# Audio tower on one core: patches embedded without their norm, which a rank-two term adds behind the product

## The reference

```python
x = layer_norm(x, g1, b1, 1e-6)              # 448 rows x 1024
x = einsum('bpd,dh->bph', x, W) + b          # W: 1024 x 512
h = layer_norm(x, g2, b2, 1e-6)
h = h + attention(_layernorm(h))             # 16 heads of 128, causal
h = h + ffn(_layernorm(h))                   # rows rounded to fp8, 512 x 512
```

## Time and profile before

| | |
|---|---|
| median of 3 runs | 266.8 us (266.61 to 266.83) |
| profiled execution, its own time | 268.16 us |
| its span, first to last instruction | 266.4 us |
| PE busy | 256.4 us (96%) |
| DVE busy | 159.5 us (60%) |
| ACT busy | 124.8 us (47%) |
| mean granted TensorE clock | 0.991 |

### The profile page before, as it was taken

One profiled execution on the slowest core, in us unless ns is written; L12 is line 12 of the kernel. 1 busy time (PEld: TensorE's weight loads), 2 busy tenths in 40 slices (PEclk: granted clock), 3 DMA queues, 4 the chain that ended last, 5 costly groups with the idle time before them and its releaser, 6 DMA issues.

```text
span 266.4 us, 3864 instructions
## 1 busy us (share of the span) xinstructions
PE 256.4 (96%) x1434; PEld 219.8 (83%) x1434; DVE 159.5 (60%) x325; ACT 124.8 (47%) x215; POOL 0.2 (0%) x4
## 2 busy tenths in 40 slices
PE   7799999899899999999999999999999999999994
PEld 6344446898799999999999999999999999998672
DVE  5268996833926903872394269138722967934884
ACT  2666964354534542534362435325443642546680
POOL 0000000000000000000000000000000000000000
PEclk9999999999999999999999999999999999999888
DMA  6999030033071053023305210530240020000004
GB/s 180 332 277 387 11 119 0 2 123 113 0 253 65 2 197 118 1 60 137 118 0 171 64 80 0 197 118 0 43 153 0 2 79 0 2 0 0 0 4 138
DMA packets 7627, 23.63 MB, mean 89 GB/s; under 512 B 1261, under 2 KB 1725, under 8 KB 7488
## 3 DMA queue, kind: packets, MB, share of 16 engines
q1 hardware_dynamic: 7616, 23.48, 26.9%
HBM read 22.56 MB, written 0.92 MB: 88 GB/s over the span
## 4 chain that ended last, share of the span: by engine, by line
PE 88%; DMA 4%; DVE 3%; SPq 2%; issue 1%; ACT 1%; DVEq 0%; ACTq 0%
PE bank L315 14%; PE bank L317 14%; PE bank L316 14%; PE acc L459 9%; PE acc L350 9%; PE bank L434 5%; PE bank L443 5%; PE acc L463 4%; DMA tokw_raw<-tok_w 4%; PE acc L653 3%; PE bank L449 3%; PE bank L426 2%; SPq L248 2%; PE bank L523 2%; PE bank L639 1%; PE bank L339 1%
## 5 line engine op out<-in xcount | busy, mean ns | idle before, releaser
L315 PE MATMUL bank<-ht_hi,qkvw_hi 128*128 128x448 f32 (+1 forms) x192 | 69.4, 362 | 0.9 <-issue 0.9
L317 PE MATMUL bank<-ht_hi,qkvw_lo 128*128 128x448 f32 (+1 forms) x192 | 69.1, 360 | 0.0
L316 PE MATMUL bank<-ht_lo,qkvw_hi 128*128 128x448 f32 (+1 forms) x192 | 69.0, 359 | 0.0
L948 DVE TENSOR_TENSOR qkvw_lo<-raw_qkv,qkvw_hi 128x1536 fp32r<-128x1536 f32 x16 | 28.1, 1754 | 35.6 <-ACT qkvw_hi L685 35.6
L315 PEld LDWEIGHTS bank<-ht_hi,qkvw_hi 128*128 128x128 f32 x192 | 36.1, 188 | 3.9 <-issue 1.3
L317 PEld LDWEIGHTS bank<-ht_hi,qkvw_lo 128*128 128x128 f32 x192 | 36.1, 188 | 2.7
L316 PEld LDWEIGHTS bank<-ht_lo,qkvw_hi 128*128 128x128 f32 x192 | 36.1, 188 | 2.6
L350 PE MATMUL acc<-tokw_raw,xt 128*112 128x512 f32 x64 | 29.7, 600 | 1.7 <-DMA tokw_raw<-tok_w 1.3
L685 ACT CAST qkvw_hi<-raw_qkv 128x1536 fp32r<-128x1536 f32 x16 | 23.5, 1477 | 0.0
L350 PEld LDWEIGHTS acc<-tokw_raw,xt 128*112 128x112 f32 x64 | 10.4, 176 | 15.4 <-issue 9.6
L1154 DVE COPY prob_t<-bank 112x448 f32<-112x448 f32 x8 | 5.0, 625 | 29.0 <-PE bank L426 29.0
(11 more groups left out here) (148 smaller groups left out, 396.5 us busy)
## 6 DMA issues: line engine op xcount, KB each, us to landing
raw_qkv<-heads_w SPq DMA_DIRECT2D x16, 768.0 KB, 4.3
raw_out<-heads_w SPq DMA_DIRECT2D x16, 256.0 KB, 4.5
tokw_raw<-tok_w SPq DMA_DIRECT2D x4, 512.0 KB, 7.4
x_in<-patches SPq DMA_DIRECT2D x3, 448.0 KB, 11.2
ffnw_raw<-ffn_w SPq DMA_DIRECT2D x1, 1024.0 KB, 16.4
out<-h_sb SPq DMA_DIRECT2D x3, 224.0 KB, 2.6
x_in<-patches SPq DMA_DIRECT2D x2, 224.0 KB, 3.0
g_row<-tok_g SPq DMA_DIRECT2D x1, 224.0 KB, 10.7
```

What stands on the lines that cost most here:

```text
L315: nc.tensor.matmul(ps, hi, whi, start=first, stop=False, skip_group_check=True)
L316: nc.tensor.matmul(ps, hi, wlo, start=False, stop=False, skip_group_check=True)
L317: return nc.tensor.matmul(ps, lo, whi, start=False, stop=last, skip_group_check=True)
L948: return nc.vector.tensor_tensor(dst, src, hi.bitcast(F32), ALU.subtract)
```

## The change

The patches are no longer normalised before the product. With m and s the mean and the deviation of a row, the embedding times s is

    (x g1) W  -  m (g1 W)  +  s (b1 W + b)

so PE turns the raw patches, ACT lays only g1 on, and the two last terms are added by one more product, of a column of row statistics with two rows of gains (`recentre`). What stands in `acc[t]` is the embedding times s; the next norm takes that factor out again, its epsilon being scaled by s squared (`x_eps_4`).

- **Gains.** Two spare columns of `xt` hold g1 and b1 for tile 0 (`SPARE` = 114 rows in the product), so that rows 112 and 113 of `acc[0]` become g1 W and b1 W; `gains_done` adds b to the latter. They are kept in high and low parts (`gains_hi` on ACT, `gains_lo` on VectorE).
- **Statistics.** -m (ACT) and s (VectorE) of two tiles at a time are laid into `stat_cols`, turned by PE (`stat_transposes`) and split as well (`stat_hi`, `stat_lo`). The roots of the patches' variances are taken for two tiles at a time (`patch_roots`), and `patch_sigmas` on VectorE waits for them.
- **Order.** The loads, and the work of the front on all engines, stand in another order. Every rsqrt now starts from a root of ACT, and each tile's second and third norm are made in one go (`stream_norms(t)`). The warm-up products at the start are 6 and 2 rather than 14.

```diff
-WARM_START, WARM_STATS, WARM_RSTD, WARM_SCALE = 14, 2, 3, 3
+WARM_START, WARM_STATS, WARM_RSTD, WARM_SCALE = 6, 2, 3, 3
...
+SPARE = TR + 2
+G_ROW, G_AGAIN, G_LO = 96, 64, 32
+STAT_COLS = slice(G_LO + TR - 96, 128, 32)
+SIGMA_COLS = slice(G_LO + TR - 96 + 1, 128, 32)
...
-            for c, landed in ((slice(0, 512), x_landed[0]), (slice(512, IN_DIM), x0_rest_landed)):
-                load(x_in[:, 0, c], patches[0][:, c], landed)
+            load(x_in[:, 0, 0:512], patches[0][:, 0:512], x_landed[0])
             load(ident_sb[:], ident, ident_landed)
             load(g1_col[:], tok_g1, cols_landed)
+            load(x_in[:, 0, 512:IN_DIM], patches[0][:, 512:IN_DIM], x0_rest_landed)
+            load_tokw(0)
             load(b1_col[:], tok_b1, cols_landed)
-            load_tokw(0)
+            load_tokw(1)
+            load_tokw(2)
             load(tok_b_raw[:], tok_b, tok_b_landed)
-            load_tokw(1)
+            load_tokw(3)
             load(x_in[:, 1, :], patches[1], x_landed[1])
-            load_tokw(2)
-            load_tokw(3)
             load(x_in[:, 2, :], patches[2], x_landed[2])
             load(x_in[:, 3, :], patches[3], x_landed[3])
...
-                    pe.wait_ge(x0_half_normed, 1)
-                else:
-                    pe.wait_ge(x_normed, t + 1)
+                pe.wait_ge(x_landed[t], 16)
...
-            def embed(t, half, within=None):
-                for k in range(half * KIN // 2, (half + 1) * KIN // 2):
+            def embed(t, ahead_of):
+                m = SPARE if t == 0 else TR
+                if t == 0:
+                    pe.wait_ge(spare_ok, 2)
+                if t == TILES - 1:
+                    pe.wait_ge(stat_lo_ok, 2)
+                for k in range(KIN):
+                    if k in ahead_of:
+                        ahead_of[k]()
                     for i, (first_chunk, _) in enumerate(TOKW_PIECES):
                         if t == 0 and k == first_chunk:
                             pe.wait_ge(tokw_landed[i], 16)
                     pe.wait_ge(xt_ok, KIN * t + k + 1)
-                    nc.tensor.matmul(acc[t][0:TR, :], xt[:, t % 2, k * TR:(k + 1) * TR], tokw_raw[:, k, :],
+                    nc.tensor.matmul(acc[t][0:m, :], xt[:, t % 2, k * SPARE:k * SPARE + m], tokw_raw[:, k, :],
                                      start=(k == 0), stop=False, skip_group_check=True)
...
+            def gains_done():
+                pe.wait_ge(tok_b_lo_ok, 1)
+                pe.wait_ge(ones_ok, 3)
+                nc.tensor.matmul(acc[0][0:SPARE, :], bias_row[:], tok_b_split[:], start=False, stop=False,
+                                 skip_group_check=True).then_inc(gain_ps, 1)
+            def stat_transposes(pair):
+                pe.wait_ge(sigma_ok, pair + 1)
+                pe.wait_ge(negmean_ok, pair + 1)
+                if pair == 1:
+                    pe.wait_ge(stat_lo_ok, 1)
+                for t in range(2 * pair, 2 * pair + 2):
+                    last = nc.tensor.transpose(acc[TILES - 1][:, t * TR:(t + 1) * TR], stat_cols[:, t, :],
+                                               ident_sb[0:TR, 0:TR])
+                last.then_inc(stat_ps, 1)
+            def recentre(t):
+                pe.wait_ge(gain_lo_ok, 1)
+                pe.wait_ge(stat_lo_ok, t // 2 + 1)
+                nc.tensor.matmul(acc[t][0:TR, :], stat_t[:, t, :], gain_rows[:], start=False, stop=True,
+                                 skip_group_check=True).then_inc(tok_ps, 1)
...
-            pe.wait_ge(ones_ok, 2)
+            pe.wait_ge(ones_ok, 1)
             keep_warm(WARM_START, acc[TILES - 1])
             patch_transposes(0)
-            for t in range(TILES):
-                embed(t, 0)
-                if t == 0:
-                    embed(t, 1, within=lambda: patch_transposes(1))
-                    continue
-                if t + 1 < TILES:
-                    patch_transposes(t + 1)
-                else:
-                    stream_transposes(1)
-                embed(t, 1)
-                if t == TILES - 2:
-                    stream_transposes(0)
+            keep_warm(2, acc[TILES - 1])
+            embed(0, {KIN - 2: lambda: patch_transposes(1)})
+            gains_done()
+            embed(1, {2: lambda: stat_transposes(0), 4: lambda: patch_transposes(2), 6: lambda: recentre(0)})
+            recentre(1)
+            embed(2, {2: lambda: stat_transposes(1), 4: lambda: patch_transposes(3)})
+            recentre(2)
+            stream_transposes(0)
+            embed(3, {4: lambda: stream_transposes(1)})
+            recentre(3)
             stream_transposes(2)
...
+            def patch_evacuate(t, half):
+                act.wait_ge(xt_ps, 2 * t + half + 1)
+                if t == 2 and half == 0:
+                    act.wait_ge(gain_ps, 1)
+                if t == 3 and half == 0:
+                    act.wait_ge(tok_ps, 2)
+                for k in range(half * KIN // 2, (half + 1) * KIN // 2):
+                    nc.scalar.mul(xt[:, t % 2, k * SPARE:k * SPARE + TR],
+                                  bank[2 * (t % 2) + half][:, k % 4 * TR:(k % 4 + 1) * TR],
+                                  g1_col[:, k:k + 1]).then_inc(xt_ok, 1)
+            def patch_roots(pair):
...
+                nc.scalar.activation(root[:, t], moments[:, t, 1], ACT.Sqrt, bias=eps_4[:, 0:1],
+                                     scale=0.25).then_inc(x_root_ok, 1)
+                act.wait_ge(cleared, 3)
+                nc.scalar.mul(stat_cols[:, t, STAT_COLS], moments[:, t, 0:1].to_broadcast([TR, 2, 3]),
+                              -1.0).then_inc(negmean_ok, 1)
...
-            take_root(0)
-            normalise(0, slice(IN_DIM // 2, IN_DIM))
+            act.wait_ge(eps_ok, 2)
+            nc.scalar.activation(last_root[:, 0:1], eps_4[:, 0:1], ACT.Sqrt)
             act.wait_ge(cols_landed, 32)
-            patch_evacuate(0)
+            patch_evacuate(0, 0)
+            patch_evacuate(0, 1)
             act.wait_ge(tok_b_landed, 16)
             hi_part(tok_b_split[:], tok_b_raw[:]).then_inc(tok_b_hi_ok, 1)
-            take_root(1)
-            normalise(1)
-            patch_evacuate(1, between=lambda: take_root(2))
-            normalise(2)
-            take_root(3)
-            take_root(TILES)
-            normalise(3)
-            patch_evacuate(2)
+            patch_evacuate(1, 0)
+            patch_roots(0)
+            patch_evacuate(1, 1)
+            gains_hi()
+            stat_hi(0)
+            patch_evacuate(2, 0)
+            patch_evacuate(2, 1)
+            patch_roots(1)
+            token_root(0)
+            stat_hi(1)
             split_qkv(0, 0)
+            stream_root(0)
+            normalise_stream(0)
+            token_root(1)
+            patch_evacuate(3, 0)
+            patch_evacuate(3, 1)
+            stream_root(1)
+            stream_evacuate(0)
+            normalise_stream(1)
             split_qkv(0, 1)
+            token_root(2)
+            stream_evacuate(1)
+            stream_root(2)
+            normalise_stream(2)
             split_out(0, 0)
-            normalise_stream(0)
-            take_root(2 * TILES + 1)
-            patch_evacuate(3)
-            stream_evacuate(0)
-            take_root(TILES + 2)
-            normalise_stream(1)
-            stream_evacuate(1)
-            take_root(2 * TILES + 2)
-            normalise_stream(2)
+            token_root(3)
             stream_evacuate(2)
-            take_root(TILES + 3)
             keep_stream(2)
             act.wait_ge(late_landed, 64)
             hi_part(ffn_b_split[:], ffn_b_raw[:]).then_inc(ffn_b_hi_ok, 1)
-            take_root(2 * TILES + 3)
+            stream_root(3)
             stream_evacuate(3)
...
+            def rsqrt_from_root(c, minus_v4):
+                v, y, n = vscaled[:, c:c + 1], rstd[:, c:c + 1], newton[:, c:c + 1]
+                link(nc.vector.reciprocal(y, root[:, c:c + 1]))
+                need(minus_v4)
+                link(nc.vector.scalar_tensor_tensor(out=n, in0=y, scalar=v, in1=y, op0=ALU.mult, op1=ALU.mult))
+                link(nc.vector.scalar_tensor_tensor(out=y, in0=n, scalar=3.0, in1=y, op0=ALU.add, op1=ALU.mult))
...
+            def patch_sigmas(pair):
+                t = slice(2 * pair, 2 * pair + 2)
+                dve.wait_ge(x_var_ok, 2 * pair + 2)
+                nc.vector.tensor_scalar(x_eps_4[:, t], moments[:, t, 1], LN_EPS, 4.0 * LN_EPS,
+                                        ALU.add, ALU.mult).then_inc(x_eps_ok, 1)
+                dve.wait_ge(x_root_ok, pair + 1)
+                link(nc.vector.reciprocal(sigma_rec[:, t], root[:, t]))
...
+            def stream_norms(t, between=None):
+                c, p = TILES + t, 2 * TILES + t
+                dve.wait_ge(tok_ps, t + 1)
+                moments_of(c, [acc[t][0:TR, :]], tok_var_ok)
+                dve.wait_ge(tok_var_ok, t + 1)
+                centred_step = mark(nc.vector.scalar_tensor_tensor(
```

(44 more changed lines are left out.)

235 lines of the change are left out of this document (83 added, 152 removed).

## The result

The changed kernel takes 272.6 us (median of 4 runs, 270.68 to 274.64) against 266.81 of before; ratio 1.0187, interval 1.0138 to 1.0236. It is slower, as forecast, and by 5.8 us where 2.0 were forecast. The four executions lie in two pairs, 270.68 and 271.11 at a mean granted clock of 0.998 and 0.999, and 274.09 and 274.64 at 0.987. The profiled one is of the first pair: 271.11 us, span 269.2.

A forecast was written before the change was run, and what follows sets the result against it. PE, busy 256.4 of 266.4 us, was taken as the bound, with only the front changing. PE's and the norms' paths met at 51.1 against 49.18: +2.0 on the 266.8 median gave 268.8 us, range 267.4 to 270.6.

The forecast's parts named there:

- The train of norms: VectorE's norms of tiles 0 to 3 in the front: start at 26.6 us instead of 21.90, 4.7 later.
- Lengths: VectorE's time in the norms of tiles 0, 1 and 2: 6.1, 6.3 and 6.6 us.
- PE's wait behind `recentre(3)`: PE stands idle 1.5 us before turning tile 2 of the stream, at 45.9 to 46.0 instead of 43.38.
- From landing to the end of the front: PE's and the norms' paths meet at 51.1 against 49.18: +1.9 to +2.0 us up to line 523.
- PE's added work: One more `recentre` product (0.59) and statistics transposes (0.4) in the front: PE alone +0.9 us.
- Rival 1: Only PE's added work in the front shows: +0.9, 267.7 us; chance 0.08.
- The landing of tile 1: Tile 1's patches, loaded behind all of W, land at 15.64, where W's fourth piece did; the rearrangement gains 0.1 us.
- Taking 1.4 us off both sides: Whole-kernel time: the profiled execution lay 1.4 above the median, so 270.2 became a median of 268.8 us.
- PE ready for tile 1 by then: Front: first product by about 8.5, tile 0 with over 2 us to spare before tile 1 lands.
- b1's column, put at nothing: Front loads: landing behind W's first piece, it holds back the first copies, yet the first product starts by about 8.5.
- Rival 3: PE runs tile 0's products at 1.2 GHz after the shorter warm-up: +3.1 on top, 271.9 us; chance 0.09.
- The loop: The loop over heads behind the front keeps its order, so the front's gain or loss is the whole change.

The follow-up runs named there:

- b_again1: Kernel before the change, run again unchanged for a profile: 267.22 us.
- e4: Changed kernel with the norms brought forward: PE finishes accumulator 0 before turning tile 2, VectorE norms tile 0 before later patch statistics; 269.39 us, ratio 1.0052.
- e8: Changed kernel with only the VectorE and ScalarE half of e4's reordering, PE's order kept: 271.54 us, ratio 1.0125.
- e3: Changed kernel with b1's column loaded ahead of W's first piece: 271.7 us, ratio 1.0168.
- e6: Changed kernel with the edits of e3 and e4 together: 270.0 us, ratio 1.0065.
- e10: e6 plus an unused 32-byte tile behind `bias_row`, which moves the loop's tiles: ratio 0.9991 against the kernel before.
- e13: e10 with tile 1's patches loaded between W's third and fourth pieces: 267.83 us, ratio 1.0029 against the kernel before.
- a_again1: Changed kernel, run again unchanged for a profile: 274.73 us at a mean clock of 0.987.
- e12: Changed kernel plus only the unused 32-byte tile behind `bias_row`: ratio 1.0125 against the kernel before.

## Why the prediction was wrong in size

Taken by its own steps:

- **The train of norms: right, its start in part by luck.** Start 26.6 said, 27.07 measured: tile 1 landed 1.2 later than said, and ACT's eight copies took 2.06 where I had 2.77. Lengths 6.1, 6.3, 6.6 said, 6.10, 6.83, 6.60 measured. PE's wait behind `recentre(3)` 1.5 said, 1.79 measured. From landing to the end of the front: +1.9 to +2.0 said, +1.86 measured (36.89 against 35.03; 1.63 against b_again1's 35.26). e4 takes it back. The late start as such is not in the chain that ended last; tile 0's stretch is, through the statistics that PE turns at 30.16 and the root at 32.00 (29.5 and a wait of 0.9 in the prediction).
- **PE's added work: smaller than said, and covered.** `recentre` takes 0.23 in the chain where I had the 0.59 of a bias product, two transposes of statistics 0.2; the train, not PE, is what ends last. Rival 1 falls.
- **The landing of tile 1: the step that failed.** "With ring order I put its landing where that was: 15.64." It was 16.84, so tile 1's turning, and with it line 557, came later: 53.96 and not 52.9. And 15.64 was itself late: in the seven profiles of the kernel before and its variants W's fourth piece landed at 13.90 to 15.64, 14.34 in the middle. In the eight with the changed order of loads tile 1 landed at 14.80 to 16.84, 16.26 in the middle. Taking 1.4 us off both sides, from the profiled execution to the median, treated as common what the change alone makes late: 1.9 us of the median. Part of it is perhaps b1's column between two pieces of W: in the three runs with it ahead, tile 1 landed at 14.46 to 15.41, each time earliest of its chip. One profile on each of three chips doesn't settle it.
- **PE ready for tile 1 by then: failed beside it.** The forecast had tile 0's six products done when tile 1 landed ("tile 0 has over 2 us to spare"). PE was through with them at 16.62, so a landing at 15.64 would have given this execution only the 0.22 us that PE waited. Two terms made it late. b1's column, put at nothing, landed at 9.24 (6.8 to 8.1 in the seven others with this order of loads), and the first product started at 9.73, not 8.5. And the clock: the products started at 1.2 GHz, by their weight loads (below) up to about 12.7. Four records took 3.3 us until 13.02, against 1.7 at full clock.
- **The clock: a rival, and no term in the sum.** Rival 3 put the fall at a cold start and let the wait for tile 1 swallow it. In the profiled execution the wait did swallow it, with 0.22 us to spare. It didn't in the runs with an earlier landing: in e8, e4, e3, e6, e10 and e13 PE turned tile 1 at 0.15, 0.42, 0.61, 1.00, 1.44 and 1.71 us behind its landing, being busy with tile 0 until then. e10 shows it (below). The kernel before, with 14 warm-up products and not 6 and 2, has weight loads of 0.18 from its first product on. No run has the changed order with 14 warm-up products, so that this number of products is the cause, and what the front would gain, is open. A fall in the middle of the front, behind that very wait or behind the one ahead of tile 2's transposes, was not in the prediction at all: it cost 1.6 in a_again1 and 1.25 in e3.
- **The loop: "the loop over heads keeps its order", so nothing was to change there.** Its order is kept and its addresses are not: 0.38 us for each slow step.

The weight loads of the changed kernel's first products, at the lower and at the upper level:

```profile
12.41 0.32 PEld L371 LDWEIGHTS acc<-tokw_raw,xt 128*114 128x114 f32 x1 [0.54 <-issue]
13.02 0.18 PEld L371 LDWEIGHTS acc<-tokw_raw,xt 128*114 128x114 f32 x1 [0.30 <-issue]
```

The same for e10_both_layout, with the landing of tile 1 (VectorE's row) and PE's products and turning around it:

```profile
7.94 8.13 PE L372 MATMUL acc<-tokw_raw,xt 128*114 128x512 f32 x12 [0.80 <-issue]
13.17 0.32 PEld L372 LDWEIGHTS acc<-tokw_raw,xt 128*114 128x114 f32 x1 [0.54 <-issue]
13.76 0.18 PEld L372 LDWEIGHTS acc<-tokw_raw,xt 128*114 128x114 f32 x1 [0.28 <-issue]
14.46 1.29 DVE L1017 BATCH_NORM_STATS2 stats<-x_in 112x6 f32<-112x512 f32 x2 [2.29 <-DMA x_in<-patches]
15.90 0.93 PE L354 MATMUL bank<-ident_sb,x_in 112*128 112x112 f32 x8
```

PEclk reads 1.00 in windows there: the column says nothing of the level before the first rise.

The sum for one execution closes: a_again1 has a span of 272.9, b_again1 265.4. The end of the front is 5.44 later: landing 2.17, train 1.63 (36.89 against 35.26), fall 1.64. The five steps and those beside them, from the first turned values to the last before the loop ends (66.44 to 242.93 against 61.14 to 235.89), are 1.74 longer, and the rest 0.3. That is 7.5. The pair of executions at 270.7 to 271.1 has landing and train; those at 274.1 to 274.6 fit with a fall and slow steps besides, which for these two is worked out and not seen. The median lies between. For it an estimate from the middles: landings of 14.34 and 16.26 and 35.2 and 36.9 us from there make the front 3.6 us later, where 2.0 were forecast; the other 2.2 of the 5.8 us are left for falls and slow steps, which the forecast had at nothing.

## What to carry to other kernels

A landing read from one profile is one draw: take several before a term rests on it, and ask what the median of before contains. Ask too whether the engine that waits would have been ready any earlier: here PE was through only 0.22 us before the late tile landed, and with earlier landings its slow first products set the start. A new wait of PE has a second price beside its length, what the clock loses behind it. New tiles in front of a loop move its operands; when a loop without a new instruction gets slower, try 32 bytes of padding before looking for a cause in the schedule.

## What was not expected of the hardware

- PE's 448-column products keep one of two distances, 0.203 or 0.207 us, through whole steps of the loop, at a granted clock of 1.00. Addresses of tiles bear on it (33 slow steps of 50 in the changed layout, 1 of 25 in that of before, 3 of 5 for the kernel before in the changed layout). What they do to PE is open, and so is why e13 has three slow steps where e10 and e12 have none.
- A granted clock of 0.5 for 3.4 us behind waits of 1.58 to 2.10 us, in four of ten cases; the end of the front came 1.25 (e3) and 1.6 us (a_again1) later by it. One at 251 us cost about 0.1.
- One and the same order of loads lands its tile 1 anywhere in 2.0 us (14.80 to 16.84).
